# A scan kernel with packed last channels, layer norms applied by ScalarE, statistics taken first, and an earlier input load

## What is computed

```python
w = _ln(windows_of(_gn(x)), ln1_w, ln1_b)      # 7x7 windows: 49 tokens in a row
def step(h, xb):                                # the scan over the 49 tokens
    h = xb + h @ A
    return (h, h)
hs = scan(step, 0, w @ Bm)
xr = hs @ Cm
y  = gelu(_ln(xr, ln2_w, ln2_b) @ W1 + b1) @ W2 + b2      # 192 -> 768 -> 192
x  = x + xr + y
```

## Time and profile before

| | us |
|---|---|
| median of three runs | 4774.01 (4771.63 to 4776.94) |
| profiled execution, its own time | 4771.56 |
| its span | 4769.8 |
| PE busy | 4471.3 (94%) |
| DVE busy | 4085.7 (86%) |
| POOL busy | 2642.9 (55%) |
| ACT busy | 2351.8 (49%) |

### The profile page before, as it was taken

One profiled execution on the slowest core, in us unless ns is written; L12 is line 12 of the kernel. 1 busy time (PEld: TensorE's weight loads), 2 busy tenths in 40 slices (PEclk: granted clock), 3 DMA queues, 4 the chain that ended last, 5 costly groups with the idle time before them and its releaser, 6 DMA issues. The chain is left out here.

```text
span 4769.8 us, 122473 instructions
## 1 busy us (share of the span) xinstructions
PE 4471.3 (94%) x42440; PEld 3822.0 (80%) x42440; DVE 4085.7 (86%) x7841; ACT 2351.8 (49%) x4594; POOL 2642.9 (55%) x1714
## 2 busy tenths in 40 slices
PE   0599999999999999999969999999999999999998
PEld 0488888888888888888857888888888888888887
DVE  6798888888888888888838888888888888888887
ACT  0244444444444444444415555555555555555555
POOL 1245555455545554555536666666666666666665
PEclk9999999999999999999969999999999999999999
DMA  8011111111111111111112222222222222222222
GB/s 341 21 38 38 39 39 41 37 39 39 41 37 39 39 41 38 38 39 39 37 46 79 80 78 79 81 81 77 80 79 81 77 81 78 82 80 78 79 81 65
DMA packets 398996, 310.66 MB, mean 65 GB/s; under 512 B 140011, under 2 KB 397243, under 8 KB 397755
## 3 DMA queue, kind: packets, MB, share of 16 engines
q1 hardware_dynamic: 396212, 307.89, 21.9%
q10 hardware_dynamic: 2736, 2.14, 0.1%
HBM read 145.48 MB, written 87.33 MB: 49 GB/s over the span
## 5 line engine op out<-in xcount | busy, mean ns | idle before, releaser
L885 POOL TENSOR_TENSOR E<-E,ri 128x588 f32<-128x588 f32 x512 | 802.8, 1568 | 781.5 <-DVE ri L1092 781.5
L604 PE MATMUL ps_o<-w,g_hi 128*128 128x384 f32 x2352 | 709.7, 365 | 5.9 <-DVE g_lo L544 4.1
L416 ACT ACTIVATE gF<-ps_g,b1f 128x512 f32<-128x512 f32 x588 | 404.6, 688 | 392.8 <-PE ps_g L635 390.7
L604 PE MATMUL ps_o<-w,g_lo 128*128 128x192 f32 x2352 | 534.5, 254 | 0.0
L969 ACT ACTIVATE PT<-ps_t 98x588 f32<-98x588 f32 x512 | 338.9, 662 | 395.6 <-PE ps_t L1216 395.6
L1082 DVE SCALAR_TENSOR_TENSOR L<-ps_s,bias 128x588 f32<-128x588 f32 x512 | 394.6, 771 | 152.3 <-PE ps_s L1208 144.2
L1216 PE MATMUL ps_t<-ident,E 128*98 128x128 f32 x3072 | 441.8, 280 | 78.5 <-POOL E L885 78.4
L443 POOL TENSOR_TENSOR res<-xt,b2b 128x768 f32<-128x768 f32 x98 | 181.0, 1847 | 591.1 <-DVE x L492 591.1
L1216 PEld LDWEIGHTS ps_t<-ident,E 128*98 128x98 f32 x3072 | 313.8, 128 | 233.4 <-POOL E L885 198.1
L402 ACT ACTIVATE h_hi<-ps_h,hbias 128x512 fp32r<-128x512 f32 x196 | 123.1, 679 | 703.6 <-PE ps_h L619 703.6
L1208 PE MATMUL ps_s<-Kp,Q 64*64 64x196 f32 x6144 | 455.1, 342 | 2.7 <-DMA Kp<-K 2.7
(11 more groups left out here) (203 smaller groups left out, 12238.8 us busy)
## 6 DMA issues: line engine op xcount, KB each, us to landing
xs<-in_x SPq DMA_DIRECT2D x8, 4704.0 KB, 22.3
xt<-in_x SPq DMA_DIRECT2D x98, 384.0 KB, 3.4
x_cells<-x SPq DMA_DIRECT2D x784, 48.0 KB
xb<-x_cells SPq DMA_DIRECT2D x128, 294.0 KB
Vx<-V SPq DMA_DIRECT2D x512, 73.5 KB
out<-yo SPq DMA_DIRECT2D x128, 294.0 KB
Kp<-K SPq DMA_DIRECT2D x512, 49.0 KB, 1.8
gnr<-gn_rows SPq DMA_DIRECT2D x128, 192.0 KB
```

The lines of the kernel that those rows point to most:

```text
L416: act.activation(gF[f % 4][:, :], ps_g[:, f % 2, :], ACT.Gelu, bias=b1f[:, f:f + 1]).then_inc(s_gelu, 1)
L604: last = pe.matmul(dst, g[:, f, P * k:P * (k + 1)], w, start=(f == 0 and i == 0), stop=(f == FT - 1 and i == 1))
L885: pool.tensor_tensor(e, e, ri[p][:, :].unsqueeze(2).to_broadcast([P, HEADS, T]), ALU.mult)\
```

## The change

**Packed last channels.** The last 64 state channels were computed with 64-column weights, in ten products: for each of B and A the pairs (upper weight, upper data), (upper weight, lower data), (lower weight, upper data) for the first 128 input channels and two more for the last 64. Now the 64 lower-part weight columns lie beside the 64 upper-part ones, so that one product with 128 weight columns gives both sums, one in partitions 0 to 63 and the other in 64 to 127 of `ps_h[:, 1, :]`. Six products do the work of ten. The two halves must then be added: ACT copies the lower half out (`h_low`), DVE adds both and the bias (`h_b`), ACT makes the upper part of that, DVE the lower.

**Layer norms applied by ScalarE.** The four-instruction steps L537 and L569 leave DVE. ACT does them as `Identity(rstd * x + offset)`, with scale and bias read per partition; POOL makes the offset -mean * rstd in one more small instruction after each power, and DVE makes -mean in one more small instruction.

**Statistics first.** The first layer norm's statistics stand directly behind the group norm on DVE, ahead of the lower parts of y; on POOL the power and the new product stand ahead of `res`.

**Load.** SP loads `xt` for step n + 3 in slot n, ahead of the stores of that slot, once `res` of step n + 1 has been read; in the loop the stores no longer wait for `s_x1` on their own, since POOL's `res` waits for the same count.

The second of ACT's two new groups, the one on `yb`, stands behind the upper parts of `xn`, last in the slot. The hardware loop is one t shorter, and two more slots are written out. In the attention one index of a bias column in an ACT instruction changes (`3 - m` to `m`); the number and the shapes of the instructions stay.

```diff
@@ class Split @@
+            def packed_terms(self, data_hi, data_lo):
+                both = slice(self.cols - self.beside, self.cols + self.beside)
+                a_hi, _, b_hi, _ = self.parts
+                return ((a_hi[:, both], data_hi[:, 0, :]), (a_hi[:, both], data_lo[:, :]), (b_hi[:, both], data_hi[:, 1, :]))
...
@@ SP @@
                 def slot(t, c):
                     n = CHUNKS * t + c
-                    if there(n + 2):
-                        upto(sp, s_res, n + 1)
-                        sp.dma_start(xt[c][:, :, :],
+                    d, u = (1 - c), (t if c else t - 1)
+                    if there(n + 3):
+                        upto(sp, s_res, n + 2)
+                        load(t + 1 + c, 1 - c)
...
                         sp.wait_ge(s_init, 1)
-                        sp.wait_ge(s_x1, n)
+                        if isinstance(n, int):
+                            sp.wait_ge(s_x1, n)
...
@@ ACT @@
-                        for k, rows in enumerate((P, CB)):
-                            last = act.activation(h_hi[d][0:rows, k, :], ps_h[0:rows, k, :], ACT.Identity,
-                                                  bias=hbias[0:rows, k:k + 1])
-                        last.then_inc(s_hh, 1)
+                        act.activation(h_low[0:CB, :], ps_h[CB:P, 1, :], ACT.Copy).then_inc(s_hc, 1)
+                        act.activation(h_hi[d][:, 0, :], ps_h[:, 0, :], ACT.Identity, bias=hbias[:, 0:1])
                     if there(n):
                         act.wait_ge(s_t2, n + 1)
                         upper_parts(y_hi, ps_g).then_inc(s_yh, 1)
+                    if there(n + 2):
+                        act.wait_ge(s_of1, n + 3)
+                        for k in range(TPC):
+                            last = act.activation(xn[c][:, k, :], xn[c][:, k, :], ACT.Identity,
+                                                  bias=ofa[:, k:k + 1], scale=rsa[:, k:k + 1])
+                        last.then_inc(s_xn, 1)
+                    if there(n + 1):
+                        act.wait_ge(s_hb, n + 2)
+                        act.activation(h_hi[d][0:CB, 1, :], h_b[0:CB, :], ACT.Copy).then_inc(s_hh, 1)
...
+                    if there(n + 1):
+                        act.wait_ge(s_of2, n + 2)
+                        act.wait_ge(s_rsum, n + 2)
+                        upto(act, s_t2, n + 1)
+                        for k in range(TPC):
+                            last = act.activation(yb[:, k, :], tok_tile(ps_r, k), ACT.Identity,
+                                                  bias=ofb[:, k:k + 1], scale=rsb[:, k:k + 1])
+                        last.then_inc(s_y, 1)
...
@@ POOL @@
+                        pool.wait_ge(s_rs1, n + 3)
+                        pool.tensor_tensor(ofa[:, :], nma[:, :], rsa[:, :], ALU.mult).then_inc(s_of1, 1)
...
                         pool.tensor_tensor(rsb[:, :], veb[:, :], neg_half[:, :], ALU.pow).then_inc(s_rs2, 1)
+                        pool.wait_ge(s_rs2, n + 2)
+                        pool.tensor_tensor(ofb[:, :], nmb[:, :], rsb[:, :], ALU.mult).then_inc(s_of2, 1)
...
@@ DVE @@
+                        dve.tensor_scalar(nma[:, :], mva[:, :, 0], -1.0, None, ALU.mult)
...
+                        dve.wait_ge(s_hc, n + 2)
+                        dve.scalar_tensor_tensor(out=h_b[0:CB, :], in0=ps_h[0:CB, 1, :], scalar=hbias[0:CB, 1:2],
+                                                 in1=h_low[0:CB, :], op0=ALU.add, op1=ALU.add).then_inc(s_hb, 1)
...
@@ PE @@
+                        for m, terms in enumerate(((*W_B.terms(xn_hi[d], xn_lo[d], first),
+                                                    *W_A.terms(h_hi[d], h_lo[d], first)),
+                                                   (*W_B.packed_terms(xn_hi[d], xn_lo[d]),
+                                                    *W_A.packed_terms(h_hi[d], h_lo[d])))):
                             for k, (w, v) in enumerate(terms):
-                                last = pe.matmul(ps_h[0:rows, m, :], w, v, start=(k == 0), stop=(k == len(terms) - 1))
+                                last = pe.matmul(ps_h[:, m, :], w, v, start=(k == 0), stop=(k == len(terms) - 1))
```

More of the change, by code:

```diff
@@ L162, in _ @@
                         for t in range(2):
-                            act.activation(parts.parts[2 * t][:, :], full[:, t, :], ACT.Copy)
+                            act.activation(parts.upper(t), full[:, t, :], ACT.Copy)
                     act.activation(w2[:, :, 0, :], raw_2[:, :, :], ACT.Copy).then_inc(s_wh, 1)
@@ L175, in _ @@
                         for t in range(2):
-                            pool.tensor_tensor(parts.parts[2 * t + 1][:, :], full[:, t, :],
-                                               parts.parts[2 * t][:, :], ALU.subtract)
+                            pool.tensor_tensor(parts.lower(t), full[:, t, :], parts.upper(t), ALU.subtract)
+                            if parts.beside:
+                                pool.tensor_tensor(parts.lower_beside(t), full[:, t, P:C], parts.upper(t)[:, P:C],
+                                                   ALU.subtract)
                     pool.tensor_tensor(w2[:, :, 1, :], raw_2[:, :, :], w2[:, :, 0, :], ALU.subtract)
@@ L281, in build @@
             h_lo = [sb(f"h_lo{b}", [P, NTOK], f32r) for b in range(2)]
+            h_low, h_b = sb("h_low", [P, NTOK]), sb("h_b", [P, NTOK])
             yb = sb("yb", [P, TPC, C])
@@ L333, in slots @@
                     slot(n // 2, n % 2)
-                with engine.Fori(2, T - 1) as t:
+                with engine.Fori(2, T - 2) as t:
                     slot(t, 0)
                     slot(t, 1)
-                for n in range(STEPS - 2, STEPS + 1):
+                for n in range(STEPS - 4, STEPS + 1):
                     slot(n // 2, n % 2)
@@ L367, in slot @@
                             parts = [(x1[d][base:base + WINS, k, :],
-                                      x1_cells[rows, imgs.start + 2 * k, cols, bass.ds(u, 1), :]
-                                      .rearrange("r w t c -> r w (t c)")) for k in range(TPC)]
+                                       x1_cells[rows, imgs.start + 2 * k, cols, bass.ds(u, 1), :]
+                                       .rearrange("r w t c -> r w (t c)")) for k in range(TPC)]
                             parts += [(x1[d][base:base + CELLS, :, :],
@@ L380, in slot @@
                                 sp.dma_start(dst, src).then_inc(s_st[d], 16)
+                load(0, 0)
                 slots(sp, slot)
@@ L474, in _, with lower_parts @@
             def _(dve):
[L475 removed]
+                def lower_parts(hi, lo, full):
                     for k, rows, dst in ((0, P, lo[:, :]), (1, CB, hi[CB:P, 1, :])):
[L478 to L483 removed]
+                        last = dve.tensor_tensor(dst, full[0:rows, k, :], hi[0:rows, k, :], ALU.subtract)
                     return last
@@ L533, in slot @@
                                 .then_inc(s_gld, 1)
-                    if there(n + 2):
-                        dve.wait_ge(s_rs1, n + 3)
-                        for k in range(TPC):
-                            last = dve.tensor_scalar(xn[c][:, k, :], xn[c][:, k, :], mva[:, k, 0:1], rsa[:, k:k + 1],
-                                                     ALU.subtract, ALU.mult)
-                        last.then_inc(s_xn, 1)
                     if there(n):
@@ L947, in evacuated @@
                         last = act.activation(K[0:rows, k, :, :], full[0:rows], ACT.Identity,
-                                              bias=bqkv[0:rows, 3 - m:4 - m])
+                                              bias=bqkv[0:rows, m:m + 1])
                     last.then_inc(s_qkm, 1)
```

77 lines of the change are left out of this document (40 added, 37 removed).

## The result

The changed kernel takes 4854.75 us (median of four runs, 4853.77 to 4855.64), the kernel before 4772.82 in the same comparison (4770.23 to 4776.94). The ratio is 1.017, with a 95% interval from 1.0158 to 1.0182: **slower by 82 us**. The prediction said 4850, in a range from 4745 to 4900.

A forecast was written before the change was run, and what follows sets the result against it. It took PE and an almost equally long DVE and POOL loop to bound the kernel. 22.78 + 0.18 + 0.66 = 23.62 us a step, 94 x 0.84 = +79 us, gave 4850 us, range 4745 to 4900.

The forecast's parts named there:

- PE's list: PE's own products in a scan step: ten become six at 0.23 us each, so 0.92 us shorter a step.
- The order of DVE and POOL: In a scan step, DVE's group norm multiply arrives inside POOL's first sum and gets in before the second, ending W+17.08.
- The subtraction: DVE's group norm subtraction, held by POOL's second sum, ends at W+19.65, no earlier than the 19.79 before.
- ACT's term: At W1's third group: ACT's layer norm on `xn` delays the first GELU, so PE waits, +0.66 us a step.
- The term before W1: Ahead of W1, the first MLP layer: statistics and small instructions delay y's lower parts, +0.18 us a step.
- a second loop: In the kernel before: a chain through DVE and POOL, almost as long as PE's step of 22.78 us.
- the wait at W1 (0.15 + 0.11): Kernel before, at W1: PE waits about 0.15 us for y's lower parts; its first product takes 0.50 instead of 0.39.
- PE stays the bound, faster: Rival: the multiply precedes POOL's first sum, W1 is ready before PE; 21.6 us a step, 4661 us; chance 0.17.
- The deciding point: Whether DVE's multiply comes before POOL's first sum or inside it; 0.5 us of DVE or POOL timing decides.
- the two other rivals: POOL's small product at 0.8 to 0.9 us: no change, chance 0.10; about 0.5 or more: 4900 to 4930, chance 0.07.

The follow-up runs named there:

- e2: Kernel before, with POOL's two long sums moved to the start of the next slot, behind DVE's subtraction: 4776.31 us.
- e9: Kernel before, with DVE taking y's two lower parts ahead of the state's two: 4773.66 us.
- e1: Changed kernel, with POOL's two long sums moved one slot on, behind the first layer norm's small product: 4639.64 us.
- e6: Changed kernel, with the first layer norm back on DVE, its statistics behind the state's lower parts and POOL's power behind `res`: 4823.84 us.
- e7: e6 with the first layer norm's statistics directly behind `x1_half`, ahead of the state's lower parts: 4704.0 us.

## Why the prediction was right, and where it was off

**Right, with its sizes.** All times here are medians over the steps, counted from W1; to compare with the prediction's, 0.81 us has to come off those behind the third group of W1, by which the last `g_hi` is later (W+9.81, and 9.00 before). PE's list: 4 x 0.23 = 0.92 us shorter, measured 0.91 (scan sum to the transposes of y, 4.59 and 3.68). The order of DVE and POOL: the multiply arrives inside the first sum (said W+14.93, measured 15.84 - 0.81 = 15.03) and gets in between the sums; said end W+17.08, measured 17.92 - 0.81 = 17.11. The subtraction: said 19.65, measured 20.44 - 0.81 = 19.63, and 19.79 before. POOL's small product 0.20 for 0.19, ACT's four instructions 1.87 for 1.8, the first GELU's bank free 0.66 us after the third group wanted it, as said. The Trainium skill (SBUF — State Buffer, Who interferes with whom) says that issue order decides who blocks; the trace agrees for the multiply, issued before the second sum, which cost that sum 0.7 us (2.57 against 1.86) and did not wait for it.

**Off in two terms.** A step grew by 0.94 us, not 0.84. ACT's term is 0.81 us where 0.66 was said. The third group of W1 starts 0.67 later, as said; then comes the slower restart after that wait, 0.11 us between the first two products, which the prediction had counted at W1 but left out here (before there was one such place in W1, now there are two); the last 0.03 was not traced. The term before W1 is 23.72 - 0.81 - 22.78 = 0.13 where 0.18 was said. 22.78 + 0.13 + 0.81 = 23.72, as measured. The two errors have opposite signs: with ACT's term alone put right, the sum would have been 14 us higher. In the whole launch 93 of the 97 distances between starts of W1 grew by 0.93 us on average, 86.5 together; the first two and the last two together shrank by 1.9 (the first is 22.68 us where it was 24.33, the last but one 22.32 where it was 22.78). That makes the 84.7 us, where the prediction had 94 x 0.84 = 79.

**Wrong in the account of before.** "So a second loop has almost the same length as PE's, and it goes through DVE and POOL" is true, but there were more of that length: the one from ACT's upper parts of the state (e2), and DVE's own list through the layer norm (e9). That the wait at W1 (0.15 + 0.11) was all PE's waiting was wrong too: 0.19 more stood before the second layer. Neither changed the sum, since the change takes both away and its own waits are longer.

**The rivals.** "PE stays the bound, faster", at 21.6 us a step and 4661 us, is nearly e1, though by another cause: 21.43 and 4639.64. The deciding point was where it was put, the order of the multiply and POOL's sums. The small product took neither 0.4 nor 0.8 us, so that the two other rivals had no ground.

## What to carry to other kernels

When an engine's work is moved off, follow the instructions behind it to their new times and ask what each meets there: here DVE came sooner to two operations with both inputs in SBUF, met two POOL sums, and was done hardly sooner than before (0.16 us). In the kernel before such a hold cost nothing; with 0.92 us less on PE's list, and the statistics and ACT's layer norm hung behind it, it turned a gain of 1.35 us a step into a loss of 0.94, until the sums, whose results the scan does not need, were put elsewhere. An edit's worth depends on what else binds: the early load was worth nothing in the kernel before, 25 us in the changed one and 181 us once the sums were away. And where several chains end together, an experiment that shortens one shows nothing; cutting a step by the starts of the bounding engine's groups shows where the wait went.

## What the runs showed that was not expected

- A DVE operation whose only tile input is in SBUF is held by POOL as well: the layer norm's `tensor_scalar` on 192 columns, with two operands per partition, takes 0.374 us alone and up to 1.41 beside POOL's `g_lo`, so that four took 3.2 us (before, e6, e7).
- DVE holds POOL just as well: POOL's second sum took 2.57 us instead of 1.86, and in e6 the power on four elements per partition, beside DVE's `g_lo`, 1.43 instead of 1.02.
- A POOL product on four elements per partition takes 0.20 us where the power takes 1.02, and was cheap enough to stand in a chain.
- A restart of PE after a wait costs 0.11 us beyond the wait, at a granted clock of 1.00.
